# An MoE tile loop with earlier table building, a ring of 16, and a projection one unit later in the second attention

## The reference

```
x = layernorm(x + latent_attention(x))      # 16 heads of 64, rotary, causal, softmax
x = layernorm(x + moe(x))                   # 16 experts, the best 4 for each token
x = layernorm(x + attention(x))             # 16 heads of 8
x = layernorm(x + two_layers(x))            # local attention + gated MLP, twice
```

```
logits = -dist2(x, keys) + x @ rw.T + rb          # 16 numbers a token
topv, topi = top_k(logits, 4);  w = softmax(topv)
hidden = gelu(x @ w1[e].T + b1[e])                # 128 -> 512
out[e] = hidden @ w2[e].T + b2[e]                 # 512 -> 128
fused  = sum over the 4 chosen experts of w * out[e]
```

## Time and profile before

| what | value |
|---|---|
| runs | 1426.07, 1435.71, 1432.06 us; median 1432.06 us |
| profiled execution | 1431.9 us, its span 1430.1 us |
| busy | PE 91%, DVE 66%, ACT 61%, POOL 42% of the span |
| TensorE clock, mean granted | 0.958 of full |
| tile loop | about 445 to 640 us |
| attention with heads of 8 | about 667 to 935 us |

### The profile page before, as it was taken

One profiled execution on the slowest core, in us unless ns is written; L12 is line 12 of the kernel. 1 busy time (PEld: TensorE's weight loads), 2 busy tenths in 40 slices (PEclk: granted clock), 3 DMA queues, 4 the chain that ended last, 5 costly groups with the idle time before them and its releaser, 6 DMA issues. The chain is left out here.

```text
span 1430.1 us, 29192 instructions
## 1 busy us (share of the span) xinstructions
PE 1302.6 (91%) x9813; PEld 884.3 (62%) x9813; DVE 947.3 (66%) x2523; ACT 877.4 (61%) x2316; POOL 601.4 (42%) x581
## 2 busy tenths in 40 slices
PE   7999999999998789986989999979999888999986
PEld 5777777777777789974333333246666655666654
DVE  1777887788885523355788888267777546777754
ACT  1656655655655445552677776467777547777741
POOL 1222325435436564441000000277777227777721
PEclk9999999999999989996899999699999999999998
DMA  9980000000012666853000000000000000000001
GB/s 305 326 258 1 2 2 24 9 2 24 10 48 72 148 181 190 254 168 116 1 1 1 2 1 1 0 1 1 2 2 1 1 0 1 1 1 1 1 1 30
DMA packets 53045, 78.28 MB, mean 55 GB/s; under 512 B 19607, under 2 KB 35094, under 8 KB 52038
## 3 DMA queue, kind: packets, MB, share of 16 engines
q1 hardware_dynamic: 48326, 66.97, 16.2%
q0 software_dynamic: 4576, 9.45, 1.9%
HBM read 65.91 MB, written 32.79 MB: 69 GB/s over the span
## 5 line engine op out<-in xcount | busy, mean ns | idle before, releaser
L626 ACT ACTIVATE a_prob<-ps,a_negmax 128x512 f32<-128x512 f32 (+3 forms) x256 | 133.2, 524 | 120.2 <-DVE a_negmax L783 117.4
L500 POOL TENSOR_TENSOR a_qk_r<-a_qk_c,a_qk_s 128x512 f32<-128x512 f32 x64 | 81.6, 1274 | 256.5 <-DVE a_qk_s L773 256.5
L1786 ACT ACTIVATE c_sb_pT<-ps 128x512 f32<-128x512 f32 x256 | 137.4, 600 | 71.0 <-PE ps L2001 69.9
L1856 DVE TENSOR_REDUCE c_sb_negmax<-ps 128x1 f32<-128x512 f32 x240 | 152.4, 683 | 37.0 <-PE ps L1986 36.7
L2383 ACT ACTIVATE l_sb_prob<-ps,l_sb_negmax,l_sb_rn 128x192 f32<-128x192 f32 (+1 forms) x256 | 124.1, 499 | 46.8 <-DVE l_sb_negmax L2485 46.8
L663 ACT ACTIVATE m_hid<-ps,m_w 128x128 f32<-128x128 f32 x316 | 89.9, 368 | 81.0 <-PE ps L1351 80.9
L783 DVE CUSTOM_DVE_ANT_0 ps<-ps,a_cmask 128x512 f32<-128x512 f32 (+3 forms) x256 | 120.4, 512 | 18.8 <-PE ps L1208 18.8
L2294 POOL TENSOR_TENSOR c_sb_pT<-c_sb_pT,l_sb_tab_s 128x512 f32<-128x512 f32 x64 | 110.4, 1746 | 22.1 <-ACT c_sb_pT L2341 19.4
L559 POOL DMA_INDIRECT m_y_d<-m_yo,m_xr x79 | 77.3, 978 | 76.0 <-DVE m_yo L1029 67.6
L1208 PE MATMUL ps<-a_qkT 64*128 64x256 f32 (+3 forms) x512 | 104.6, 486 | 2.2 <-ACT a_qkT L619 1.1
L1231 PEld LDWEIGHTS ps<-a_probT,a_lat 128*64 128x64 f32 x1280 | 67.9, 136 | 58.4 <-issue 30.2
(11 more groups left out here) (298 smaller groups left out, 3223.3 us busy)
## 6 DMA issues: line engine op xcount, KB each, us to landing
m_w<-w1T SPq DMA_DIRECT2D x79, 258.0 KB, 3.3
m_rows_d<-pad SPq DMA_DIRECT2D x17, 1040.0 KB, 36.6
m_xr<-m_rows_d SPq DMA_DIRECT2D x79, 65.0 KB, 2.8
m_w<-w2T SPq DMA_DIRECT2D x1, 4096.0 KB, 14.2
m_y<-m_y_d SPq DMA_DIRECT2D x16, 256.0 KB, 4.1
pre_wqkv<-wqkv SPq DMA_DIRECT2D x6, 256.0 KB
m_y_d<-m_yo,m_xr POOLq DMA_INDIRECT x79, 3.6
keep_x<-x SPq DMA_DIRECT2D x1, 1024.0 KB, 9.0
```

The costliest lines, as they stand in the source:

```text
L626: nc.scalar.activation(prob[:, u % 4, 0:width(p)], score_ps(n, p, j)[:, 0:width(p)], ACT.Exp, bias=negmax[:, u:u + 1], scale=-1.0, accum_o ...
L1786: nc.scalar.activation(pT[:, m % 2, g + i, t, :], ps[:, pair(exp_turn(e)).start + i, :], ACT.Exp, scale=SCALE).then_inc(exp_done, 1)
L1856: nc.vector.tensor_reduce(negmax[:, m % 2, t, g + i:g + i + 1], ps[:, pair(max_turn(k)).start + i, :], AX.X, ALU.max, negate=True).then_in ...
```

## The change

- `RING` goes from 12 to 16: `xr` and `yo` have four more places each, and a ring place must be free only 16 tiles later.
- The second table is begun at tile 0 instead of tile 1, and written at tile 4 instead of tile 6; `mark_used(1)` follows at tile 6. SP's `table_out(1)` moves from j = 8 to j = 9, behind `ids_in(3)`, and `table_in(1)` from 10 to 11.
- The last sequence: ACT normalises one of its four parts behind each of the tiles 0 to 3 instead of all four behind tile 1; PE's `turn`, `route`, `ranks` and everything behind them on DVE and ACT come two tiles later; POOL copies its rows in two halves at tiles 5 and 6, and sends them from tile 14 instead of 12.
- The third table is written at tile 18 instead of 17; SP's `table_out(2)` moves from j = 20 to 24 and `table_in(2)` from 23 to 26.
- In `attention1`, `project(m + 3, 0)` stands behind unit 5 instead of 4 on PE, and `leading(m + 3, 0)` behind the exponentials of unit 5 instead of 4 (and so behind `copy_o`) on ACT.

```diff
-RING = 12
+RING = 16
@@ SP
-            if j == 8:
-                table_out(1)
             if j == 9:
                 ids_in(LASTB)
-            if j == 10:
+                table_out(1)
+            if j == 11:
                 table_in(1)
...
-            if j == 20:
+            if j == 24:
                 table_out(2)
-            if j == 23:
+            if j == 26:
                 table_in(2)
@@ POOL
-            if j == 3:
-                copy_rows(LASTB, range(TPB))
+            if j in (5, 6):
+                copy_rows(LASTB, range(2 * j - 10, 2 * j - 8))
             send_out(j)
-            if 12 <= j < 18:
-                send(LASTB, 3 * (j - 12), min(3 * (j - 12) + 3, TPB * TOPK))
+            if 14 <= j < 20:
+                send(LASTB, 3 * (j - 14), min(3 * (j - 14) + 3, TPB * TOPK))
@@ ACT
-            if j == 1:
-                for i in range(TPB):
-                    normalise(LASTB, i)
-            if j == 3:
+            if j < TPB:
+                normalise(LASTB, j)
+            if j == 5:
                 copy_xT(LASTB)
-            if j == 6:
+            if j == 8:
                 exp_top(LASTB)
...
@@ PE
-            if j == 2:
+            if j == 4:
                 turn(LASTB)
-            if j == 4:
+            if j == 6:
                 route(LASTB)
-            if j == 10:
+            if j == 12:
                 ranks(LASTB)
@@ attention1, ACT
             exps(e + 4)
-            if m + 3 < NQ:
-                leading(m + 3, 0)
             if m == NQ - 1:
                 local.copy_qk(0)
             if m:
                 copy_o(m - 1)
             exps(e + 5)
+            if m + 3 < NQ:
+                leading(m + 3, 0)
@@ attention1, PE
-                if r == 4 and m + 3 < NQ:
+                if r == 5 and m + 3 < NQ:
                     project(m + 3, 0)
```

More of the change, by code:

```diff
@@ L1118, in _ @@
             weigh(j)
+            if j == 0:
+                count_tiles(1)
             if j == 1:
-                count_tiles(1)
+                limits(1)
             if j == 2:
-                limits(1)
+                scan(1)
             if j == 3:
-                scan(1)
+                place_tiles(1)
             if j == 4:
-                place_tiles(1)
-            if j == 5:
+                write_table(1)
+            if j == 6:
+                mark_used(1)
+            if j == 7:
                 take_logits(LASTB)
                 tops_of(LASTB)
-            if j == 6:
-                write_table(1)
-            if j == 7:
+            if j == 8:
                 places_of(LASTB)
-            if j == 8:
+            if j == 9:
                 choose(LASTB)
-            if j == 9:
+            if j == 10:
                 tally(LASTB)
                 weights(LASTB)
-            if j == 11:
+            if j == 13:
                 take_ranks(LASTB)
                 slots(LASTB)
-            if j == 12:
-                mark_used(1)
-            if j == 13:
+            if j == 14:
                 count_tiles(2)
-            if j == 14:
+            if j == 15:
                 limits(2)
-            if j == 15:
+            if j == 16:
                 scan(2)
-            if j == 16:
+            if j == 17:
                 place_tiles(2)
-            if j == 17:
+            if j == 18:
                 write_table(2)
-            if j == 18:
+            if j == 19:
                 spread_gates(LASTB)
```

## The result

| | before | after |
|---|---|---|
| median of the runs | 1431.12 us (4 runs) | 1415.66 us (4 runs, 1415.02 to 1416.2) |
| span of the profiled execution | 1430.1 us | 1414.4 us |
| tile loop, first to last `weigh` | 186.5 us | 181.0 us |
| attention, first to last maxima | 225.0 us | 214.8 us |
| time at half clock, whole span | 120 us | 104 us |

The ratio is 0.989, 95% interval 0.9855 to 0.9929: 15.5 us less, where 2.4 had been forecast. In the two profiles the loop gives 5.5 us and the attention 10.2. The rest cancels: the stage ahead of the loop is 3.8 us shorter after (a difference of 0 to 5 us that also stands between runs of kernels that are alike up to there), and the part behind the last maxima is 3.8 us longer. The last two rows of the table sum the granted clock over windows of 1 us.

The account below looks back on a forecast made before the run. PE was taken to bound the tile loop, held up at `up(8)` and `up(20)`. 9.9 - 6.6 plus 11.4 less 10.8 + 2.5 gave 1.4 us, with 1.0 in the attention 2.4: 1429.7 us, range 1422 to 1438.

Parts of the forecast that it names:

- Start of the loop: Tile loop's start: with ACT's normalisations spread out, `down(1)` is late next; 0 us, between 2.1 gained and 2 lost.
- First stall: PE's wait at `up(8)` for its w1: 9.9 us go, but a new stall at `up(9)` costs 6.6 us.
- rival 4: Tile loop: the clock stays up in the new stall at `up(9)`, 2.2 us earlier at `up(16)`, 1427.5 us; chance 0.15.
- Second stall: PE's wait at `up(20)`, with SP held at `table_out(2)`, goes: 11.4 us, 2 of them by RING 16.
- Tile 28: SP waits at j = 28 for all 64 sends: PE stands 10.8 us at `up(28)`, plus 2.5 us of clock.
- The loop together: Whole tile loop: 1.4 us gained, between 6.3 gained and 4.0 lost.
- The attention: Attention rounds with the projection behind unit 5: 0.1 us a round, 1 us in 13 rounds.
- the whole wait: Attention: PE's wait for DVE before the projection, 4 us, as upper bound; as a rival 1426.6 us, chance 0.12.
- Rival 3: Tile loop: sends hidden, no wait at tile 28, waits at `up(8)` and `up(20)` gone: 15.7 us gained, 1416; chance 0.05.
- two conditions named as proof of error: Tile loop and attention: forecast wrong if PE doesn't stand at tile 28, or if a round shortens by 0.3 us.

Follow-up runs that it names:

- ACT's half alone: Kernel before with only `leading` moved behind `copy_o` and unit 5's exponentials on ACT, PE's projection left behind unit 4: 1432.79 us, ratio 1.003.
- full-array filler: Kernel before plus one unread 128x128 by 512 product ahead of unit 6's exponent products in each of 13 rounds: 1423.72 us against 1431.51, ratio 0.994.
- narrow filler: Kernel before with unit 6's first exponent products run three times in the 13 rounds with a projection: 1430.86 us against 1432.58, ratio 0.998.

## Why the prediction was wrong

By its own steps:

- **Start of the loop, 0.** The gelu behind the first normalisation was named as late next, and `down(1)` does wait, 2.89 us. What was not counted is that the clock falls there for 3.4 us (450.5 to 453.9), about 2 us lost. But this loss and the next term are one: PE would otherwise have waited for tile 9.
- **First stall, 9.9 us gone, 6.6 new.** `up(8)` waits for nothing, as forecast. `up(9)` was put at 471.2, 23.9 us behind `up(1)` (447.30 before); it came 23.0 behind. So the sum was right within 1 us, but with luck, for its first link was not there: SP did not stand at `ids_in` for the 48th send. It came there only at 457.10, straight behind `fetch_w1(8)`, which had waited for the gelus that the stall at `down(1)` held back, and then stood 1.1 us at `table_out(1)` for the table. The w1 of tile 9 went out 18.1 us behind `up(1)`, forecast 19.9, and took 4.9 us to its `up` instead of 4.0. The split was wrong: 1.11 us of wait at `up(9)`, not 4.4, and the clock stayed up, as in rival 4. That was luck as well: the bound taken from the rows, that 2.11 us left the clock up, is one draw, and in four of the seven profiles with that wait the clock fell behind it. The run with a later normalisation has the picture forecast: SP stands for the send until 461.38, 14.6 us behind `up(1)` (forecast 14.75), and `up(9)` waits 4.12 us, with the clock down. `up(16)` comes 37.8 us behind `up(1)`, forecast 40.0.
- **Second stall gone.** Right, there is none at `up(20)`. That RING 16 has a part of 2 us in it was not shown by the times: alone it gave 1.6 us (interval −0.3 to 6 us), and 2.8 within the new order. The traces speak for it: with the ring alone the stretch from `up(20)` to `up(28)` is 1.9 us shorter than before.
- **Tile 28.** The place, the cause and the clock dip were right; the time from first to last send is 25.26 us, as forecast. The size was off, `up(28)` comes 71.6 us behind `up(1)` where 75.6 was forecast. 2.1 of the 4.0 come from the first send, 39.7 behind `up(1)` instead of 41.8. The other 2.0 lie between the last send and `up(28)`: landing 3.0 us instead of 4.0, the w1 0.6 us behind the rows instead of 1.3, its arrival 3.1 instead of 3.3. The clock costs 1.8 (515.12 to 518.85 less 1.90) instead of 2.5. By the fixed cost and the bandwidth that the Trainium skill gives in "DMA: Bandwidth & Descriptors", section "Anatomy of one DMA — SWDGE (gpsimd) path", the send would have landed after 2.2 us, which is an estimate. The 3.0 us measured lie between it and the 4.0 taken.
- **The loop together.** 1.4 us forecast, 5.5 measured, within the range given (6.3 gained to 4.0 lost). Mechanism right, terms mis-sized: up to `up(28)` the forecast was 4.0 us too late.
- **The attention, 1.0 us: the step that failed.** The round's length was nearly right: 14.04 us where 14.1 to 14.2 was forecast and 14.18 was before, 1.8 us in 13 rounds. The wait for DVE is gone from L1963. But the maxima products don't wait longer for ACT, as was forecast; their waits for it fall from 25.1 us in all to 10.0. The step knew of the 0.36 us alone and left out the pause of 0.84 us behind it, which goes too. And it took one round at full clock and multiplied it by 13. In the profile before five rounds were not like it: 24 us at half clock from 688 to 842 us, which made one of them 4 us longer and the others 1.5 each, some 10 us together. The granted clock was read in the loop but in the attention only as a row of tenths, put down to its start and end. So a change of the clock in the rounds stood in the sum at nothing, and the bound of 4 us for "the whole wait" was no bound: a pause can cost more than its own length.

What was shown: the projection's move alone gives 11.9 us, with the clock at 1.00 in the rounds; one full-array product a round, and nothing moved, gives 7.8 us with the wait for DVE still in place, and no dip in the rounds; a pause put back into the new order costs 28 us. That only the length of a round at full clock counts doesn't survive them: by it they would gain 1.8 us, lose 4.3 and lose 8.2. The Trainium skill's "TensorE: Matmul & The Clock Gate", section "A second HAM failure mode: psum-queue depth-cycling", tells of a kernel in which frequent very short idle times of PE between groups of matmuls make the clock swing between its levels. The trace agrees: the clock falls here with no gap over 0.84 us in a round, among products most of which use 32 of the array's 128 rows or columns.

Rival 3 gave 1416 for want of any wait at tile 28. The time is right and the reason isn't: PE stands there for 6.44 us. The two conditions named as proof of error, no stand at tile 28 or a round shorter by 0.3 us, did not occur; the list lacked "the clock stays up in rounds where it fell".

What stays open: what part of the attention's gain belongs to each of the two pauses (0.36 and 0.84 us), since ACT's half alone left 0.36 and 0.43 and still dipped; why the dips before come in some rounds and not in others (in several profiles two or three of them begin 44.4 us apart, every third round); why 0.84 us of pauses in a round brought more of them than 1.20; and the 3.8 us ahead of the loop. The full-array filler did two things at once, it filled a pause and it gave the whole array work, and no run separates them. That the narrow products (32 rows) enter into it is argued from the narrow filler's weaker effect, 1.7 us against 7.8 with intervals that overlap, and from its dips, and not shown: that filler did not fill its pause either.

## What to carry to other kernels

Read the granted clock by stretches over every stage in which TensorE is the bound, not only where it stalls, and compare two rounds of a loop before multiplying one by their number. A short, regular pause among small matmuls may cost several times its length, as the added pause did here (8 us by the length of the rounds, 28 in all). A full-array product without use, placed in the pause, can be worth more than the work it adds. One profile's count of dips is one draw: take the gain from the times of many runs, and set several profiles of either order side by side before saying in which stage it lies. When one wait is removed in a chain of transfers, ask when the data come at all: the wait of `up(9)` only moved to where the engine stood before it.

## What the runs showed of the hardware

- The clock fell to 1.2 GHz in rounds whose longest pause was 0.84 us, and stayed low for 10 us (702.1 to 712.3) in which PE was never idle.
- The same wait did not always lower it. In the loop it fell in 6 of 8 profiles behind 2.82 to 2.89 us of idling at `down(1)`, in 4 of 7 behind 2.02 to 2.11 us at `down(2)` (the profile before is one of the three in which it stayed up), and in 1 of 3 behind 1.97 us at `up(9)`. Behind the waits of 3.07 us and more it fell each time.
- With pauses of 0.36 and 0.84 us in most rounds the mean clock from 680 to 860 us was 0.93 in one profile and 0.97 in three, with 0.36 and 0.43 it was 0.94, with 0.58 and 0.26 it was 0.87. With 0.36 and a full-array product in place of the 0.84 it was 1.00, and so it was with 0.26 alone, in the kernel after.
- Three added products of 1.1 us in the last rounds made the kernel 8.7 us faster; between 860 and 935 us its profile has 7 us at half clock, and that of the kernel after 38.
